# Gating loop: one-hots of two batches in one operation a tile, keys spread four batches ahead, indices fetched early, the chunk behind done in four parts

## The reference

```
h = (x_flat @ W_gat).reshape(M, HEADS, NUM_EXPERTS)        # 4 heads x 4 experts
src = jnp.concatenate([edge_index[0], loops]); dst = jnp.concatenate([edge_index[1], loops])
a_src = (h * att_src).sum(-1);  a_dst = (h * att_dst).sum(-1)
e = jax.nn.leaky_relu(a_src[src] + a_dst[dst], negative_slope=0.2)
e_max = jax.ops.segment_max(e, dst, num_segments=M)
ee = jnp.exp(e - e_max[dst])
denom = jax.ops.segment_sum(ee, dst, num_segments=M)
msg = h[src] * (ee / (denom[dst] + 1e-16))[:, :, None]
agg = jax.ops.segment_sum(msg, dst, num_segments=M)
```

## Time and profile before

| | us |
|---|---|
| median of 3 runs | 2589.93 (2586.99 to 2591.83) |
| the profiled execution, its own time | 2584.71 |
| its span, first to last instruction | 2582.9 |
| busy: TensorE, VectorE, ScalarE, GpSimd | 1157.9, 1877.1, 682.0, 1718.3 |
| gathers of `h`, 668 instructions, busy | 644.8 |
| one-hots, 840 operations, busy | 264.2 |

### The profile page before, as it was taken

How to read it: one execution, slowest core, us unless ns; L and a number is a source line. 1 busy time by engine, 2 the same in 40 slices (tenths; PEclk the granted TensorE clock), 3 DMA queues, 4 the chain that set the end, 5 groups by cost and what they waited for, 6 DMA issues and landing times.

```text
span 2582.9 us, 33931 instructions
## 1 busy us (share of the span) xinstructions
PE 1157.9 (45%) x12439; PEld 974.0 (38%) x12439; DVE 1877.1 (73%) x3127; ACT 682.0 (26%) x696; POOL 1718.3 (67%) x1690
## 2 busy tenths in 40 slices
PE   4662000001011100100105597888888888888386
PEld 2221000001000000000004354488888888888366
DVE  8887679997979989884327301178888888888556
ACT  1110004434335443534101011222222222222221
POOL 0005777777777777777777577777777777677370
PEclk9775555555555555555555555589999999999658
DMA  9402113333323332334314325122222222222101
GB/s 347 180 1 70 50 61 104 103 100 100 99 88 106 108 93 91 101 100 133 101 29 47 73 68 131 24 26 26 39 28 26 41 26 26 41 26 26 29 10 34
DMA packets 138177, 187.94 MB, mean 73 GB/s; under 512 B 77628, under 2 KB 96254, under 8 KB 131438
## 3 DMA queue, kind: packets, MB, share of 16 engines
q1 hardware_dynamic: 83958, 122.34, 14.6%
q0 software_dynamic: 54080, 63.61, 13.9%
HBM read 98.53 MB, written 87.32 MB: 72 GB/s over the span
## 4 chain that ended last, share of the span: by engine, by line
POOL 39%; DVE 24%; PE 17%; issue 15%; ACT 1%; DMA 1%; DVEq 0%; SPq 0%; POOLq 0%; ACTq 0%
POOL arena L739 36%; DVE arena L1379 12%; PE psum L1065 11%; DVE arena L1382 6%; POOL d_adseed L829 2%; DVE arena L1940 2%; PE psum L1026 2%; DVE arena L1989 2%; PE psum L1038 2%; POOL d_qseed L763 2%; PE psum L1110 1%; PE psum L1141 1%; DMA arena<-in_x 1%; PE psum L1055 1%; DVE arena L1927 0%
## 5 line engine op out<-in xcount | busy, mean ns | idle before, releaser
L1379 DVE TENSOR_TENSOR arena<-arena 128x512 f32<-128x512 f32 (+17 forms) x1331 | 766.6, 616 | 214.9 <-DMA arena<-d_ac,arena 65.9
L739 POOL DMA_INDIRECT arena<-d_h,arena x668 | 644.8, 965 | 227.4 <-issue 200.6
L739 POOL DMA_INDIRECT arena<-in_kv,arena x640 | 663.1, 1036 | 195.1 <-issue 195.1
L1065 PE MATMUL psum<-arena 128*128 128x128 bf16 x10080 | 606.9, 223 | 84.6 <-DVEq L1987 83.1
L1065 PEld LDWEIGHTS psum<-arena 128*128 128x128 bf16 x10080 | 593.5, 100 | 89.2 <-DVE arena L1382 86.0
L862 PE MATMUL psum<-arena 128*128 128x128 f32 (+3 forms) x402 | 92.8, 401 | 1027.4 <-DVEq L1455 800.4
L862 PEld LDWEIGHTS psum<-arena 128*128 128x128 f32 (+3 forms) x402 | 70.9, 208 | 1050.4 <-DVEq L1455 815.8
L1382 DVE TENSOR_SCALAR arena<-arena 128x512 bf16<-128x512 f16 (+8 forms) x1067 | 336.3, 373 | 71.8 <-ACT arena L1285 21.3
L1379 DVE TENSOR_TENSOR arena<-psum,arena 128x512 f32<-128x512 f32 (+2 forms) x179 | 141.2, 796 | 209.4 <-PE psum L1026 202.6
L739 POOL DMA_INDIRECT arena<-d_adst,arena x40 | 54.3, 1358 | 220.9 <-DVEq L1626 209.0
L1026 PEld LDWEIGHTS psum<-arena 128*128 128x128 f32 x512 | 113.7, 328 | 146.8 <-issue 110.5
(11 more groups left out here) (190 smaller groups left out, 1485.6 us busy)
## 6 DMA issues: line engine op xcount, KB each, us to landing
d_gs<-arena SPq DMA_DIRECT2D x32, 768.0 KB
d_as<-arena SPq DMA_DIRECT2D x20, 1152.0 KB, 4.6
d_qseed<-arena SPq DMA_DIRECT2D x5, 4096.0 KB, 31.4
arena<-d_qseed SPq DMA_DIRECT2D x20, 1024.0 KB, 5.2
arena<-d_h,arena POOLq DMA_INDIRECT x668
arena<-in_kv,arena POOLq DMA_INDIRECT x640
d_adseed<-arena SPq DMA_DIRECT2D x1, 4096.0 KB, 29.2
arena<-in_w_blocks SPq DMA_DIRECT2D x1, 2304.0 KB, 20.1
```

The source lines that it names most:

```text
L739: return pool.indirect_dma_start(out, None, table, bass.IndirectOffsetOnAxis(index[:, t:t + 1], 0))
L1065: last = nc.tensor.matmul(ps[2 + turn_of(b, m)][:, k * PICK_W:(k + 1) * PICK_W], pick_hot[turn_of(b, m)][:, t, k * P:(k + 1) * P], h_split ...
L1379: return V.tensor_tensor(o, a_, b_, op)
```

## The change

One-hots of two batches are made by one operation for each tile: `pick_all` holds the keys of two batches, 1024 wide, and so do the two sets of `pick_hot`. The second set lies in memory that has other uses before and behind the loop. The seventh batch stays single, so a chunk has 4 groups (`HOTS`): three of 8 operations on 1024 elements and one of 8 on 512. TensorE spreads the keys of a batch four batches ahead of its pick instead of two. SyncE's fetch of the next indices waits for `g_laid` instead of `g_used` and `g_rows_set` and stands ahead of the store. `maximum` and `weighted_sums` are each cut in two (`edge_scores`, `maximum`, `messages`, `weighted_sums`), and the four stand behind the takes of batches 0 to 3, one behind each. `pick_keys` of the next chunk stands ahead of the take of batch 5, and the next chunk's first pair ahead of the take of batch 6.

```diff
+HOTS = -(-BATCHES // 2)
+YT_FREE = 24
...
-        pick_all = [g.take(BATCH * P // 2, F16) for _ in range(2)]
+        pick_all = [g.take(BATCH * P, F16) for _ in range(2)]
...
-        pick_hot = [g.take(K_TILES * BATCH * P // 2, BF16).rearrange("p (t n) -> p t n", t=K_TILES) for _ in range(2)]
+        pick_hot = [[g.take(BATCH * P, BF16) for _ in range(K_TILES)]]
...
+        yT_flat = yT.rearrange("p i n -> p (i n)")
+        in_yT = YT_FREE * P // (BATCH * P)
+        pick_hot.append([yT_flat[:, t * BATCH * P:(t + 1) * BATCH * P].bitcast(BF16) for t in range(in_yT)]
+                        + [g_corr_f[:, t * BATCH * P:(t + 1) * BATCH * P].bitcast(BF16) for t in range(K_TILES - in_yT)])
...
+
+        def hot_of(w):
+
+            return min(2, BATCHES - 2 * w) * BATCH * P
...
                 for b in range(2):
                     with sp.If(it * 2 + b < n_all):
-                        sp.wait_ge(g_used, it * 2 + (b - 1))
-                        sp.wait_ge(g_rows_set, it * 2 + (b - 1))
+                        sp.wait_ge(g_laid, it * 2 + (b - 1))
                         sp.sem_inc(waits_carried, 1)
-                        sp.dma_start(gout_v[bass.ds(it * 2 + (b - 2), 1)].rearrange("c p j f -> (c p) j f"), g_rows[b]).then_inc(g_rows_out[b], 16)
                         nxt = it * 2 + b
                         sp.dma_start(g_sidx[b], gsrc_v[bass.ds(nxt, 1)].rearrange("c p j -> (c p) j")).then_inc(g_idx_in[b], 16)
                         sp.dma_start(g_didx[b], gdst_v[bass.ds(nxt, 1)].rearrange("c p j -> (c p) j")).then_inc(g_idx_in[b], 16)
                         sp.dma_start(g_dprev[b], gprev_v[bass.ds(nxt, 1)].rearrange("c p j -> (c p) j")).then_inc(g_idx_in[b], 16)
                         sp.dma_start(ad_seed[b], gseed_v[bass.ds(nxt, 1)].rearrange("c p j f -> (c p) j f")).then_inc(ad_seed_in[b], 16)
+                        sp.wait_ge(g_rows_set, it * 2 + (b - 1))
+                        sp.sem_inc(waits_carried, 1)
+                        sp.dma_start(gout_v[bass.ds(it * 2 + (b - 2), 1)].rearrange("c p j f -> (c p) j f"), g_rows[b]).then_inc(g_rows_out[b], 16)
             sp.wait_ge(g_rows_set, n_all)
             sp.sem_inc(waits_carried, 1)
...
                 last.then_inc(pick_spread, 1)
             def pick(it, b, m):
-                pe.wait_ge(pick_hot_set, chunk_count(it, b, BATCHES, m + 3))
+                pe.wait_ge(pick_hot_set, chunk_count(it, b, HOTS, m // 2 + 3))
                 pe.wait_ge(pick_taken, chunk_count(it, b, BATCHES, m + 1))
                 for k in range(BATCH):
                     for t in range(K_TILES):
                         for n in range(SPLITS):
-                            last = nc.tensor.matmul(ps[2 + turn_of(b, m)][:, k * PICK_W:(k + 1) * PICK_W], pick_hot[turn_of(b, m)][:, t, k * P:(k + 1) * P],
+                            last = nc.tensor.matmul(ps[2 + turn_of(b, m)][:, k * PICK_W:(k + 1) * PICK_W], pick_hot[m // 2 % 2][t][:, (m % 2 * BATCH + k) * P:(m % 2 * BATCH + k + 1) * P],
                                                     h_split[n][:, t * PICK_W:(t + 1) * PICK_W],
                                                     start=t == 0 and n == 0, stop=t == K_TILES - 1 and n == SPLITS - 1)
                 last.then_inc(picked, 1)
...
             pe.sem_inc(picked, 2)
             n_all = pe.value_load(g_count[0:1, 0:1], min_val=2, max_val=G_CHUNKS)
             with pe.If(n_all >= 3):
-                for m in range(2):
+                for m in range(4):
                     spread(1, 0, m)
             with nc.Fori(1, G_CHUNKS // 2, engines=[mybir.EngineType.PE], hint_back_edge=True) as it:
                 for b in range(2):
                     with pe.If(it * 2 + b < n_all):
                         for m in range(BATCHES - 2):
-                            spread(it, b, m + 2)
                             pick(it, b, m)
+                            if m + 4 < BATCHES:
+                                spread(it, b, m + 4)
                         for m in range(2):
                             pick(it, b, BATCHES - 2 + m)
                             with pe.If(it * 2 + (b + 1) < n_all):
-                                spread(it + b, 1 - b, m)
+                                for k in range(2):
+                                    spread(it + b, 1 - b, 2 * m + k)
             pe.wait_ge(exp_taken, EXPERTS_EARLY)
...
-                act.wait_ge(pick_hot_set, chunk_count(it, b, BATCHES, m + 1))
-                nc.scalar.copy(pick_all[turn_of(b, m)], ps[turn_of(b, m)][:, 0:BATCH * P]).then_inc(pick_all_set, 1)
+                act.wait_ge(pick_hot_set, chunk_count(it, b, HOTS, m // 2 + 1))
+                nc.scalar.copy(pick_all[m // 2 % 2][:, m % 2 * BATCH * P:(m % 2 + 1) * BATCH * P], ps[turn_of(b, m)][:, 0:BATCH * P]).then_inc(pick_all_set, 1)
...
             n_all = act.value_load(g_count[0:1, 0:1], min_val=2, max_val=G_CHUNKS)
             act.sem_inc(pick_all_set, 2)
             with act.If(n_all >= 3):
-                for m in range(2):
+                for m in range(4):
                     all_keys(1, 0, m)
             with act.Fori(1, G_CHUNKS // 2 + 1) as it:
                 for b in range(2):
                     with act.If(it * 2 + b < n_all):
-                        all_keys(it, b, 2)
-                        all_keys(it, b, 3)
                         lay(it, 1 - b, 1)
                         all_keys(it, b, 4)
+                        all_keys(it, b, 5)
                         weigh(it, 1 - b, 1)
-                        all_keys(it, b, 5)
+                        all_keys(it, b, 6)
                         rows(it, 1 - b, 1)
-                        all_keys(it, b, 6)
                         with act.If(it * 2 + (b + 1) < n_all):
-                            for m in range(2):
+                            for m in range(4):
                                 all_keys(it + b, 1 - b, m)
                     with act.If(it * 2 + b == n_all):
                         lay(it, 1 - b, 1)
...
-            def maximum(it, b, back, first=False):
+            def edge_scores(it, b, back):
...
+
+            def maximum(it, b, back, first=False):
...
-            def weighted_sums(it, b, back):
+            def messages(it, b, back):
+
+            def weighted_sums(it, b, back):
...
                 key_link(tt(of_, bc(pick_v[:, :, None], [P, PICKS, CANDS]), bc(iota[:, None, 0:CANDS], [P, PICKS, CANDS]), ALU.is_equal))
                 assert n_done[0] == KEY_STEPS
-            def one_hot(it, b, m):
-                dve.wait_ge(pick_all_set, chunk_count(it, b, BATCHES, m + 3))
-                dve.wait_ge(picked, chunk_count(it, b, BATCHES, m + 1))
+            def one_hot(it, b, w):
+                dve.wait_ge(pick_all_set, chunk_count(it, b, BATCHES, min(2 * w + 2, BATCHES) + 2))
+                dve.wait_ge(picked, chunk_count(it, b, BATCHES, (1, 2, 4, 6)[w]))
                 for t in range(K_TILES):
-                    ins = ts(pick_hot[turn_of(b, m)][:, t], pick_all[turn_of(b, m)], node[:, t:t + 1], ALU.is_equal)
+                    ins = ts(pick_hot[w % 2][t][:, 0:hot_of(w)], pick_all[w % 2][:, 0:hot_of(w)], node[:, t:t + 1], ALU.is_equal)
                 ins.then_inc(pick_hot_set, 1)
             def take_picked(it, b, m):
...
+            edge_scores(0, 0, 0)
+            messages(0, 0, 0)
...
-                one_hot(1, 0, 1)
...
                         p_done[0] = 0
                         flags(it, 1 - b, 1)
                         for m in range(BATCHES - 2):
-                            one_hot(it, b, m + 2)
+                            if m % 2 == 0:
+                                one_hot(it, b, m // 2 + 1)
                             take_picked(it, b, m)
-                            if m == 1:
-                                maximum(it, 1 - b, 1)
-                            if m == 2:
-                                weighted_sums(it, 1 - b, 1)
+                            if m < 4:
+                                (edge_scores, maximum, messages, weighted_sums)[m](it, 1 - b, 1)
                         for m in range(2):
                             dve.sem_inc(waits_carried, 1)
                             with dve.If(it * 2 + (b + 1) < n_all):
                                 if m == 0:
                                     pick_keys(it + b, 1 - b)
-                                one_hot(it + b, 1 - b, m)
+                                    dve.sem_inc(waits_carried, 1)
+                                else:
+                                    one_hot(it + b, 1 - b, 0)
                             take_picked(it, b, BATCHES - 2 + m)
                         picked_a_src(it, b)
                         dve.sem_inc(waits_carried, 1)
                         assert p_done[0] == PICK_STEPS
                     with dve.If(it * 2 + b == n_all):
                         flags(it, 1 - b, 1)
+                        edge_scores(it, 1 - b, 1)
                         maximum(it, 1 - b, 1)
```

(2 more changed lines are left out.)

## The result

The changed kernel takes 2578.91 us (median of 5 runs, 2577.43 to 2580.41) against 2589.93 for the kernel before, a recorded ratio of 0.9964 with a 95% interval of 0.9951 to 0.9977 (the quotient of the two medians is 0.9957). By the medians that is 11 us faster, where 35 were forecast; 2578.9 lies 2 us above the range of 2543 to 2577. The profiled execution took 2578.70 us (span 2576.9), 6.0 less than that of before.

A forecast was written before the change was run, and what follows sets the result against it. VectorE's queue with TensorE's picks bound the loop at 47.8 us a chunk; GpSimd was to bound it at 45.4. The scan 40.4 us earlier, less 5 us surcharge, gave a 35 us gain: 2554 us, range 2543 to 2577.

The forecast's parts named there:

- the surcharge: GpSimd's loop gathers wait for wide one-hots: 0.35 us a chunk, 5 us in all, of 0 to 1.3 a chunk.
- rival 4: GpSimd's gathers under wide groups each wait a whole wide operation: 49.4 us a chunk, 2609 us, slower; chance 0.07.
- One-hots of two batches: On VectorE a pair of 1024-wide one-hots takes 3.6 us and saves 1.27; three pairs save 3.8 us a chunk.
- Keys four batches ahead, VectorE's sum: VectorE loses cast waits of 1.4 and pick waits of 0.6, pays 0.9 for a late pick: 42.3 us a chunk.
- Indices fetched early: Waits for the index transfer go: GpSimd's 26.8 us in the stretch and VectorE's 0.6 us a chunk.
- The chunk behind in four parts: Its nine chained operations on VectorE stay, with only takes between them; no new wait for ScalarE or GpSimd.
- GpSimd becomes the bound: In the loop GpSimd needs 45.4 us a chunk against VectorE's 42.3, with 3 us to spare on VectorE.
- The sum: The loop's 540 gathers at 1.262 us end at 2372.0; the last scan starts at 2373.7, 40.4 us earlier.
- Rival 1: VectorE stays the loop's bound: at 4.88 us a pair it needs 46.1 us a chunk; gain 25 us, 2565; chance 0.13.
- Rival 2: TensorE's picks wait for later takes; VectorE loses 2 us twice a chunk, period 46.3, gain 22 us, 2568; chance 0.10.

The follow-up runs named there:

- experiment 1: Changed kernel with each one-hot of 1024 elements made by two operations of 512: 2559.55 us, ratio 0.988 to the kernel before.
- experiment 3: Kernel before with only SyncE's early index fetch, ahead of the store: 2588.02 us, ratio 0.9989.
- experiment 5: Changed kernel with the index fetches put back behind the store of the chunk's rows: 2587.46 us, ratio 0.9994 to the kernel before.
- experiment 6: Changed kernel with the chunk behind done in two places again instead of four: 2575.6 us, ratio 0.9957 to the kernel before.
- experiment 7: Changed kernel with only the second pair of a chunk in operations of 1024, the other pairs in 512: 2556.64 us, ratio 0.9884 to the kernel before.
- experiment 4: Changed kernel with 32 picked columns instead of 28, so four wide pairs and 32 gathers a chunk: 2546.04 us, ratio 0.9824 to the kernel before.

## Why the prediction was wrong

**The step that failed is the surcharge**, "I take 0.35 a chunk", with its bounds "between 0 and 9 x 0.146 = 1.3 us a chunk". Measured are 2.2 us a chunk. The last gather ended at 2405.33 + 0.95 = 2406.3 where the forecast, with its 5 us, had 2377.0: 29.3 us late. The scan behind came 29.5 us late, the profiled execution 29.4. The whole miss is this one term.

Two thoughts in it were wrong. First, the mean of 1.262 was read as the narrow groups' own cost, 0.4 us a chunk, and wide ones were given one of like size. Most of it was not theirs: in the kernel before the narrow groups cost the gathers 0.12 us a chunk, and 0.61 came from the 32-bit `TENSOR_TENSOR` work beside which 24 gathers took over 1 us. Second, the upper bound let a gather wait only for the 0.146 us by which an operation gets longer. How many gathers meet a wide group was forecast well (9, measured 8.3); each is held up by 0.27 us in the mean, singly by 0.1 to 0.7, where the bound allowed 0.146 and the sum took 0.04. Under narrow ones it is 0.006 to 0.011 us, so the cost of an operation grew far more than its length did. The row that showed it, was in the prediction, priced at 7 us a chunk and left to rival 4. The row was also misread. VectorE's row just ahead of it is

```profile
1159.06 4.82 DVE L1379 TENSOR_TENSOR arena<-arena 128x1024 f32<-128x1024 f32 x4
```

The gather started at 1162.73 and would have ended, at 0.94 us, at 1163.67, before the first `TENSOR_SCALAR` began at 1163.91. So it was held up by the 32-bit `TENSOR_TENSOR` first, and not all of the 1.59 us was the price of wide `TENSOR_SCALAR` work. The true price lies between the two, at 2.2, just under the 2.7 from which rival 4 decides. Bounds "from both sides" would have had to reach from nothing to the earlier trace rows for the range too.

The Trainium skill ("SBUF — State Buffer", Who interferes with whom) says that a tensor_scalar in a two-port mode and an operation of GpSimd shut each other out, the later one waiting for the whole of the other. The changed kernel's trace agrees for the wide ones: of its 92 gathers over 1 us that met them and no `TENSOR_TENSOR` of the second kind, 69 end 0.11 to 0.13 us behind the end of a wide one-hot. It agrees for the long scan, which is no such operation: 45 gathers ran beside it, and the longest took 0.947 us. That narrow operations of the same kind delay next to nothing (0.954 us in the mean in experiment 1) is the measurement's word; whoever goes by the rule alone would charge them too.

**The other steps.**
- *One-hots of two batches*: eight wide ones take 3.26 us, forecast 3.6; VectorE's work falls by 4.8 us a chunk, forecast 3.8. Right in kind, too careful in size. It bought nothing at 28 picks, as VectorE waits 5.6 us at the scan instead (forecast 2 to 3).
- *Keys four batches ahead, VectorE's sum*: right. The wait for casts is gone, and experiment 1 runs at the 46.1 us that the sum gives without wide one-hots. The late pick costs 18.3 us in 13 waits, 1.4 each where 0.9 was charged.
- *Indices fetched early*: the waits of 26.8 us went (experiment 3), and were worth next to nothing by themselves. What I had not seen is that the reordered key work needs the early fetch (experiment 5).
- *The chunk behind in four parts*, costed at nothing: right (experiment 6).
- *GpSimd becomes the bound*: right; it took the place of VectorE, at 47.7 us instead of 45.4. *The sum* without surcharge: its end of the gathers (2372.0) is right to 0.3 us in experiment 1, but its time is not, since VectorE is the bound there and the scan comes at 2386.57 instead of 2373.7.
- Rival 1 (VectorE stays the bound) did not come true in the changed kernel; its 46.1 us is the period of experiment 1. Rival 2 (a new wait for TensorE) did not come true either: the late picks cost 1.4 us a time, once a chunk.

So the expected gain was there and was given back in the same place: 31 us by the order, less 20 by the wide one-hots. That these slow the gathers is shown by experiments 1 and 7. Why a gather yields so much more at 1024 columns than at 512 was not tested and stays open.

## What to carry to other kernels

When a change makes an engine's operations fewer and longer, ask who shares something with that engine before counting its saved time: here 4.8 us a chunk saved on VectorE, which then had time to spare, cost 2.2 on GpSimd, which had none. Make operations wide only on the way to a better balance (experiment 4 pays 2.9 us a chunk for its wide one-hots and still gains 1.8% on the kernel before, since it takes gathers off GpSimd too). And when a row shows a contention in a form near to the new one, its price belongs in the range, not only among the rivals. To read such a price, look at what runs beside the instruction from its start on. And before a mean is laid on one kind of work, sort the single instructions by what each overlapped.

## What was not expected of the hardware

A 16-bit comparison of 512 columns on VectorE all but leaves GpSimd's descriptor making alone (0.954 us in the mean in experiment 1, 1.08 at most), whether eight or sixteen follow each other; one of 1024 columns stretches it to 1.211 us in the mean and as much as 1.68. The cost is 0.07 to 0.10 us for each wide operation, in seven kernels with 3 to 32 of them a chunk. Meanwhile the wide form is cheap for VectorE itself: 16 operations of 512 take 5.07 us, 8 of 1024 take 3.26.

A 32-bit `TENSOR_TENSOR` with both inputs in SBUF holds gathers up too, even one of 256 columns: 1.44 us instead of 0.94 for the gather from 1933.21. In the ten traces, the kernel before included, 226 of the loop's gathers that met no one-hot are over 1 us long, and every one of them ran beside such an operation; of the 2477 that ran beside neither a one-hot nor such an operation, not one is. With one input in PSUM, a `TENSOR_TENSOR` of 1024 columns (2.29 us) held up none of the 37 gathers beside it in the changed kernel.
